# VectorE's normalisation three groups ahead of TensorE in the finishes of a two-layer graph attention kernel

## The reference

```python
q = (x @ qw + qb).reshape(N, H, D); k = ...; v = ...      # H = 2, D = 128
alpha = einsum('ehd,ehd->eh', q[dst], k[src]) * D ** -0.5
ex = exp(alpha - segment_max(alpha, dst)[dst])
w = ex / (segment_sum(ex, dst)[dst] + 1e-16)
agg = segment_sum(w[:, :, None] * v[src], dst)
y = agg.mean(axis=1) + x @ sw + sb + x @ lin_w + lin_b
```

## Time and profile before

| | us |
|---|---|
| Median of 3 runs | 1160.34 (1159.95 to 1160.86) |
| Time of the profiled execution | 1159.89 |
| Its span, first to last instruction | 1158.1 |
| VectorE busy | 968.7 (84%) |
| TensorE busy | 949.8 (82%) |
| ScalarE busy | 843.6 (73%) |
| GpSimd busy | 754.4 (65%) |

### The profile page before, as it was taken

The page is one execution under the profiler, slowest core; times in us unless marked ns, Lnnn a source line. Parts: engine busy times, 40 slices in busy tenths (PEclk is TensorE's granted clock), DMA queues, the critical chain, the costliest instruction groups (busy, mean ns, idle before and its releaser), DMA issues.

```text
span 1158.1 us, 33825 instructions
## 1 busy us (share of the span) xinstructions
PE 949.8 (82%) x6752; PEld 759.8 (66%) x6752; DVE 968.7 (84%) x5154; ACT 843.6 (73%) x2738; POOL 754.4 (65%) x801
## 2 busy tenths in 40 slices
PE   5778888898888879889876877778888888788886
PEld 4446667676666667778854555666676667676776
DVE  6898988888788878989687787878888888889986
ACT  4566768788787878887264565768787878798766
POOL 7777777777777777720077777777777777777000
PEclk9698999999999998999897999999989999999998
DMA  5223333332332333210132232323333333332001
GB/s 165 68 81 81 90 85 87 82 91 79 82 80 82 82 83 80 80 40 1 46 83 82 72 88 73 82 81 82 80 87 80 86 82 82 78 84 71 11 1 57
DMA packets 51521, 87.15 MB, mean 75 GB/s; under 512 B 16269, under 2 KB 24739, under 8 KB 51331
## 3 DMA queue, kind: packets, MB, share of 16 engines
q0 software_dynamic: 25024, 51.30, 17.6%
q10 hardware_dynamic: 17216, 27.80, 8.4%
q1 hardware_dynamic: 9091, 5.89, 1.7%
HBM read 81.58 MB, written 3.34 MB: 73 GB/s over the span
## 4 chain that ended last, share of the span: by engine, by line
DVE 35%; PE 22%; issue 16%; DMA 11%; DVEq 5%; ACT 3%; POOL 2%; ACTq 0%; SPq 0%; POOLq 0%
DVE junk L1079 15%; PE ps L796 11%; DVE acc L1110 9%; PE ps L784 8%; DMA gathered<-h_rows,src_e 8%; DMA gathered<-in_x,src_e 2%; ACT whot L594 2%; DVEq L1079 2%; POOL gathered L455 2%; DVEq L1110 1%; DVE max_b L1150 1%; DVE hot_t L1070 1%; PE ps L896 1%; DVEq L310 1%; DVE a_end L1122 1%
## 5 line engine op out<-in xcount | busy, mean ns | idle before, releaser
L594 ACT ACTIVATE whot<-apart,below 128x128 f32<-128x128 bf16 x1664 | 562.7, 388 | 108.5 <-PE ps L796 89.0
L796 PE MATMUL ps<-gathered,whot 128*128 x3328 | 550.7, 292 | 40.4 <-DVE acc L1110 15.9
L784 PE MATMUL ps<-table,hot_t 128*128 x2496 | 434.1, 283 | 107.2 <-SPq L397 49.2
L796 PEld LDWEIGHTS ps<-gathered,whot 128*128 128x128 f32 x3328 | 443.7, 195 | 110.6 <-issue 76.6
L1079 DVE SCALAR_TENSOR_TENSOR junk<-ps,gathered 128x129 f32<-128x129 f32 x1664 | 412.9, 286 | 104.0 <-PE ps L784 65.0
L455 POOL DMA_INDIRECT gathered<-in_x,src_e x391 | 376.5, 963 | 120.9 <-issue 57.6
L455 POOL DMA_INDIRECT gathered<-h_rows,src_e x391 | 374.1, 957 | 119.1 <-issue 53.6
L1110 DVE TENSOR_TENSOR acc<-ps,acc 128x258 f32 x832 | 351.9, 423 | 35.5 <-PE ps L796 20.6
L784 PEld LDWEIGHTS ps<-table,hot_t 128*128 128x128 bf16 x2496 | 248.3, 100 | 195.5 <-issue 155.5
L578 ACT ACTIVATE apart<-col_b,ndl_e 128x128 bf16<-128x128 bf16 x742 | 286.8, 387 | 0.4 <-issue 0.3
L1079 DVE DVE_READ_ACCUMULATOR junk<-ps,gathered 128x1 f32 x1664 | 136.3, 82 | 0.0
(11 more groups left out here) (188 smaller groups left out, 552.6 us busy)
## 6 DMA issues: line engine op xcount, KB each, us to landing
dl_bc<-local_dst_rows ACTq DMA_DIRECT2D x102, 256.0 KB
gathered<-in_x,src_e POOLq DMA_INDIRECT x391
gathered<-h_rows,src_e POOLq DMA_INDIRECT x391
h_rows<-table SPq DMA_DIRECT2D x6, 256.0 KB, 2.3
out<-x_rows SPq DMA_DIRECT2D x6, 256.0 KB
dl_bc<-local_dst_rows SPq DMA_DIRECT2D x2, 256.0 KB
table<-in_L_gnn_q_w ACTq DMA_DIRECT2D x2, 128.0 KB, 3.1
table<-in_L_gnn_k_w ACTq DMA_DIRECT2D x2, 128.0 KB, 4.5
```

The source lines that it names most:

```text
L594: last = nc.scalar.activation(whot[:, c % UN, h, :], apart[:, c % UN, :], ACT.Exp, scale=FAR, bias=below[:, j % 2, h, o:o + 1])
L784: last = nc.tensor.matmul(bank_t[n % NB][:, 0:CW], hot_t[:, n // BC % 2, t % BC, :], table[:, bass.ds(b, 1), part, :].rearrange("p o c -> ...
L796: last = nc.tensor.matmul(bank_u[n % NB][:, h * C1:(h + 1) * C1], whot[:, c % UN, h, :], gathered[:, bass.ds(slot, 1), :].rearrange("p o c ...
```

## The change

`u_n` and `has` get UQ = 4 buffers instead of two. VectorE normalises groups 0, 1 and 2 ahead of its loop, and in the loop normalises group g+3 instead of group g+1. In the loop the normalisation moves from ahead of the copy of head 1 (line 1250) to behind it, which still is ahead of the skip step. The wait for a buffer now begins with group 4 and looks four groups back. Nothing else changes; no instruction is added or removed.

```diff
+UQ = 4
...
-        u_n = [tmp([G * HEADS, F]) for _ in range(2)]
+        u_n = [tmp([G * HEADS, F]) for _ in range(UQ)]
...
-        has = sb("has", [P, 2, 3, BP])
+        has = sb("has", [P, UQ, 3, BP])
...
                         nc.tensor.transpose(bank_w[0:3 * BP, g % 2 * P:(g % 2 + 1) * P],
-                                            has[:, g % 2, :, :].rearrange("p s r -> p (s r)"), ident[:, :])
+                                            has[:, g % UQ, :, :].rearrange("p s r -> p (s r)"), ident[:, :])
...
-                                                           u_n[g % 2][:, t * HEADS + h, 0:F], ident[:, :])
+                                                           u_n[g % UQ][:, t * HEADS + h, 0:F], ident[:, :])
...
-                    if g >= 2:
-                        dve.wait_ge(S["uT_tp"], m - 1)
+                    if g >= UQ:
+                        dve.wait_ge(S["uT_tp"], m - UQ + 1)
...
-                normalise(0)
+                for g in range(UQ - 1):
+                    normalise(g)
                 for g in range(NGR + 3):
-                    if g + 1 < NGR:
-                        normalise(g + 1)
                     if l == 0 and g < NGR:
                         t0, k, w = group(g)
                         dve.wait_ge(S["uT_tp"], l * NGR + g + 1)
                         if g >= 2:
                             dve.wait_ge(S["projected"], l * NGR + g - 1)
                         V.tensor_copy(uT[g % 2][:, 1, 0:w], bank_h1[:, 0:w]).then_inc(S["uT1_ready"], 1)
+                    if g + UQ - 1 < NGR:
+                        normalise(g + UQ - 1)
                     if 2 <= g < NGR + 2:
                         q = g - 2
...
```

More of the change, by code:

```diff
@@ L1234, in normalise @@
                     ln(V.reciprocal(r, d))
-                    V.tensor_scalar(has[:, g % 2, :, 0:2 * k],
+                    V.tensor_scalar(has[:, g % UQ, :, 0:2 * k],
                                     sums[:, :, F].rearrange("p (o t) -> p o t", o=1).to_broadcast([P, 3, 2 * k]),
                                     0.0, 1.0 / HEADS, ALU.is_gt, ALU.mult)
-                    V.tensor_tensor(u_n[g % 2][:, 0:2 * k, :], sums[:, :, 0:F],
+                    V.tensor_tensor(u_n[g % UQ][:, 0:2 * k, :], sums[:, :, 0:F],
                                     r.rearrange("p (t o) -> p t o", o=1).to_broadcast([P, 2 * k, F]),
                                     ALU.mult).then_inc(S["un_ready"], 1)
-                normalise(0)
+                for g in range(UQ - 1):
+                    normalise(g)
                 for g in range(NGR + 3):
-                    if g + 1 < NGR:
-                        normalise(g + 1)
                     if l == 0 and g < NGR:
```

## The result

The median is 1163.38 us over 17 runs, against 1160.86 us over 17 runs of the kernel before, taken beside them. The ratio is 1.0023, with a 95% interval of 1.0013 to 1.0033: slower, clear of no change; whether by more than the 0.2% that the prediction took as the limit is not shown, since the interval holds 1.0020. One run of the 17, at 1335.53 us, had a granted clock of 0.595 where the others had 0.935 to 0.953, so it is left out of the ratio, and the median of the other 16 is 1163.0 us. The single runs spread over 6 us before and 8 us after, and the experiments have 6 to 12 runs each (e11 one). So the profiles, which resolve hundredths of a microsecond, carry most of what follows, but each is one execution, and where TensorE's low clock falls in it differs from one to the next.

The account below looks back on a forecast made before the run. TensorE was taken to bound the first finish, VectorE the second from 1132.22. First finish +3.15, second -1.5, zeroing +0.1 sum to +1.75 us, at the median 1162.1 us; range 1160.3 to 1164.4.

Parts of the forecast that it names:

- Start of the first finish: First finish: head 1's copy for group 0 starts 1.66 us later; delay kept 1.4 us, ends 0.8 and 1.7.
- The case that the prediction worked out with the clock as before: First finish's start: if the clock returns at 561.5 as before, 0.83 us of the 1.66 us delay remains.
- The stalls at g = 2 and 3: First finish: normalisations between copy and skip step make TensorE wait 1.3 us at g = 2, 0.46 at g = 3.
- Second finish: Layer 2's finish: normalisations done earlier, blocks then bound by TensorE's 2.99 us; -1.5 us, ends -0.9 and -1.8.
- Buffers and zeroing: Both finishes, start: a buffer by itself worth nothing; doubled zeroing of `has` costs 0 to 0.2 us, taken as 0.1.
- The rule on gaps and buffers: Second finish's buffer wait: a repeating gap can mean too few buffers; by it the deeper queue is worth 1.7 us.
- (a): First finish: TensorE's clock falls once more because of the new stalls; +3.45 us, 1163.8 us; chance 0.22.
- (b): Both finishes: VectorE's relief counts in full, the first finish costs nothing; 1157.0 us; chance 0.05.
- (c): First finish: clock hides more, start delay 0.8 us, stalls together under 1 us; +0.3, 1160.7 us; chance 0.15.
- (d): Finishes: VectorE kept back by line 1231, so the change doesn't run ahead; near nothing, no chance given.
- A sign that misled: Layer 2's edge stage, untouched by edits: prediction wrong if its length changes by more than a microsecond.
- The other signs: Memset about 3 us later in the first finish; second: no buffer wait at normalisation, skip steps wait about 0.6 us.

Follow-up runs that it names:

- e11: The changed kernel profiled once more, nothing altered; first finish 31.96 us, second 36.02 us.
- e3: Changed kernel with the new order in layer 1's finish only, layer 2 one group ahead as before; ratio 1.0024 to the kernel before.
- e4: Changed kernel, but in layer 1's loop the normalisation stands behind the skip step; ratio 0.9999 to the kernel before.
- e7: Changed kernel plus dummy transposes filling TensorE's pauses (20 and 20 in layer 1, 20 and 12 in layer 2); ratio 1.0000 to the kernel before.
- e8: Order of e5 plus dummy transposes (20 and 8 in layer 1, 20 and 12 in layer 2); ratio 0.9965 to the kernel before.
- e6: Changed kernel, but layer 1 runs two groups ahead, normalisation between copy and skip step; ratio 1.0032 to the kernel before.
- e2: Changed kernel with the new order in layer 2's finish only, layer 1 one group ahead as before; ratio 0.9994 to the kernel before.
- e5: Changed kernel, but layer 1 runs two groups ahead with the normalisation behind the skip step; ratio 0.9991 to the kernel before.
- e9: Kernel before the change, with only the dummy transposes of e8 added; ratio 0.9958 to the kernel before.
- e1: Changed kernel's four buffers, but VectorE's order as before the change in both layers; ratio 1.0007 to the kernel before.
- e10: e8 with two groups ahead in layer 2 as well, instead of three; ratio 0.9953 to the kernel before.

## Why the prediction was right

The forecast was 1162.1 us and +1.75; it came out at 1163.38, +2.5 against the runs of before taken beside it, inside the range. The ratio of 1.0023 is on the slower side of the line by a hair, to which the prediction gave 0.32 against 0.63 for the other. The mechanism of each step was found. That the sizes add up so well is in part luck: F1 grew by 2.00 us in the first profile and by 2.47 in e11 instead of the forecast 3.15, and the first profile's span is +1.8 only because the edge stage of layer 2 happened to be 1.2 us longer. By its steps:

- **Start of the first finish.** The copy was forecast 1.66 us later and came 1.67 later (e3, e4, e7, e11 and the changed kernel: 5.01 in each). How much of it stays was put at 0.8 to 1.7, taken as 1.4. At group 2's transposes it was 0.4 in the changed kernel's first profile, 0.9 in e11, 1.6 in e3, and at the full clock all of it (1.67, e7 against e8). The case that the prediction worked out with the clock as before, 0.83, is borne out: in e11 the clock fell at 3.1 us, before at 3.2, and the delay is 0.86. The low end was too high: I let the low stretch begin where it did before, and it can also begin earlier, so that it eats group 0's transposes, whose end VectorE is not waiting for in the new order. TensorE's wait for the copy was 1.95 us instead of 2.7 for the same reason.
- **The stalls at g = 2 and 3.** Forecast 1.3 and 0.46, measured 1.21 and 0.35. e4 takes them out and gets 1.59 us back, e6 adds a third and F1 is at the 32.1 worked out for it. The release took 0.06 us (565.46 + 0.68 to 566.20), not the 0.14 that I had added.
- **Second finish.** Forecast -1.5, measured -1.51 from first to fifth block and -1.6 in F2 (e2, e4 and e5 have the same F2 within 0.05). Where the low stretch was 10.2 us (e6, e11), F2 was 35.8 and 36.0, and no profile shows the old order with such a stretch. And the gain holds only with a low clock at the start, when TensorE brings the first projection so late that three more normalisations fit in ahead of it. The sum took that for granted, although it noted that they end only 0.2 us before the block. e9 against e7 shows the sign turned at the full clock.
- **Buffers and zeroing.** Nothing, and 0.16 us where 0.1 was taken. The rule on gaps and buffers that the prediction took from the Trainium skill (Perfetto Trace Analysis, section Identifying Performance Opportunities) would have given 1.7 us; e1 gives 1.0007 and an F2 of 36.13 against 36.1.
- **The rivals.** (a), one more fall of the clock behind the stalls, didn't happen: in the changed kernel the clock is 1.00 from 560.5 to 579.8, with both stalls in it, and so it is around the stalls of e3, e6 and e11. The time alone doesn't tell them apart, since +2.5 lies between the forecast's +1.75 and (a)'s +3.45; these rows do. The Trainium skill's account of clock oscillation from short idling (TensorE: Matmul & The Clock Gate, section "A second HAM failure mode: psum-queue depth-cycling") is thus not borne out by stalls of 1.0 and 0.2 us here. (b) fell with e3, (c) with the waits of line 908, (d) since line 1234 never waits in either finish.
- **A sign that misled.** The prediction called itself wrong if the edge stage of layer 2 changed by more than a microsecond, and it changed by 1.20. With 2.5 us between two profiles of one kernel the sign could not carry that weight. The other signs came: the memset 2.2 us later for about 3, no wait at line 1234, waits of 0.5 us at line 1266 for 0.6.

What of the +2.5 isn't in the sum of +1.75 can't be fixed by these runs. The interval of the ratio reaches from 1.5 to 3.8 us and takes both in. The clock's low stretches of 10.2 us in F1 (e3) and F2 (e6, e11) cost 1.2 to 1.5 us where they occur, and they occurred in three of the ten finishes without dummies in which VectorE starts three groups ahead, and in none of the eight others. In those three the clock fell 1.1 to 1.4 us after the first normalisation, while TensorE stood still ahead of group 0's transposes. That pause is the same in every kernel without dummies (2.58 us, up to 1.9), so VectorE's order had not yet reached TensorE when the clock fell early, and three of ten is too few to tell from chance. Whether the order has a part in how long the clock stays low is open.

## What to carry to other kernels

Running a producer further ahead only helps if what it is moved past can wait: here one copy that frees a single bank and one skip step, both short and both awaited by the engine that is the bound, were put behind 1.67 us of work that nobody needed yet. Place the early work behind the steps that others wait for (e4, e5), and count it against the moment at which the consumer arrives, since a gain that rests on a late consumer is lost when the consumer gets faster (e9 against e7). And look at the clock before the order: keeping TensorE busy through two pauses was worth 0.4%, more than any reordering.

## What the runs showed of the hardware

Each of the 18 finishes profiled without dummies (nine profiles) starts with the same pause of TensorE, 2.58 us between the last product of the edge stage and group 0's transposes, and in each the clock came down to half (1.2 GHz). It fell 1.1 to 3.5 us after the first normalisation: four times inside that pause, otherwise during the transposes behind it or about where a second pause of 0.9 to 2.8 us began. So the fall did not need the second pause. Where the fall came at 1.8 us or later the clock was low for 6.8 us (15 finishes), where it came at 1.4 or earlier for 10.2 us (three). The same kernel showed both (e11 and the first profile of the changed one).

Shorter pauses in dense work did not bring it down: stalls of 1.04 and 0.19 us in layer 1, and one of 1.47 us in layer 2 (e7), left it at 1.00. Filling the pauses with 20 and 8 to 20 transposes of an identity, which cost about 0.12 us each at the full clock, kept it at 1.00 in both finishes as long as TensorE had work, in all four kernels with them (e7 to e10). In layer 1 this took F1 from 29.25 to 26.67 us (e5, e8).
